# Row halves for attention scores, 32x32 transposes on VectorE, expert tables in sections, and one block for all stages

## What is computed

```python
def token_diffusion(x, Wqk, Wv, Wo, tau):            # 16 heads of 16
    qk = (x @ Wqk).reshape(b, n, H, dh).transpose(0, 2, 1, 3)
    v = (x @ Wv).reshape(b, n, H, dh).transpose(0, 2, 1, 3)
    dot = einsum('bhnd,bhmd->bhnm', qk, qk)
    q2 = sum(qk * qk, axis=-1)
    logits = (2.0 * dot - q2[..., :, None] - q2[..., None, :]) / sqrt(dh) * tau
    out = einsum('bhnm,bhmd->bhnd', softmax(logits), v)
    return out.transpose(0, 2, 1, 3).reshape(b, n, d) @ Wo
# channel_diffusion: the same over channels, 8 heads of 32
x = x + token_diffusion(layernorm(x), ...) * gamma1
x = x + channel_diffusion(layernorm(x), ...) * gamma2
# experts: top 2 of 8 by softmax(x @ w_router); 256 -> 1024 -> gelu -> 256
# whole: x = x + layernorm(attention(layernorm(x))); x = x + layernorm(experts(layernorm(x)))
```

## Time and profile before

| | us |
|---|---|
| median of 3 runs | 1127.04 (1125.57 to 1129.49) |
| the profiled execution | 1118.23 |
| its span on the core | 1116.4 |
| PE busy of the span | 1032.4 (92%) |
| ACT, DVE, POOL busy | 721.1, 671.4, 384.5 |

### The profile page before, as it was taken

How to read it: one execution, slowest core, us unless ns; L and a number is a source line. 1 busy time by engine, 2 the same in 40 slices (tenths; PEclk the granted TensorE clock), 3 DMA queues, 4 the chain that set the end, 5 groups by cost and what they waited for, 6 DMA issues and landing times. The chain is left out here.

```text
span 1116.4 us, 17406 instructions
## 1 busy us (share of the span) xinstructions
PE 1032.4 (92%) x5756; PEld 702.8 (63%) x5756; DVE 671.4 (60%) x1902; ACT 721.1 (65%) x1106; POOL 384.5 (34%) x353
## 2 busy tenths in 40 slices
PE   5899999999999999998899996999999999989966
PEld 3234545555455455544588875888888888878842
DVE  5225265454735645354785777677677776679927
ACT  2797767667776766666655662676677766768804
POOL 5121030513323141224426243444433443254315
PEclk9899999999999999999999987999999999989989
DMA  7673816427082542832433133334443344446456
GB/s 267 133 246 61 264 31 204 122 84 256 18 261 73 174 150 69 275 148 91 147 100 115 62 135 123 124 133 148 147 161 119 138 143 142 151 143 224 149 215 256
DMA packets 48960, 167.47 MB, mean 150 GB/s; under 512 B 10160, under 2 KB 16688, under 8 KB 42864
## 3 DMA queue, kind: packets, MB, share of 16 engines
q1 hardware_dynamic: 38170, 136.94, 36.9%
q0 software_dynamic: 10560, 29.14, 8.2%
q10 hardware_dynamic: 150, 0.41, 0.2%
HBM read 102.74 MB, written 63.70 MB: 149 GB/s over the span
## 5 line engine op out<-in xcount | busy, mean ns | idle before, releaser
L589 ACT ACTIVATE E<-PS,VV 128x1024 f32<-128x1024 f32 x256 | 271.6, 1119 | 73.7 <-PE PS L974 72.6
L1737 PE MATMUL PH<-XP,W1P 128*128 128x512 f32 (+1 forms) x1104 | 233.1, 369 | 4.9 <-DVE HP L1678 4.5
L1737 PEld LDWEIGHTS PH<-XP,W1P 128*128 128x128 f32 x1104 | 185.8, 192 | 44.5 <-DVE HP L1678 8.1
L974 PE MATMUL PS<-OPB,OPA 102*128 102x512 bf16 x512 | 137.9, 386 | 11.4 <-DMA OPB<-norm_parts 5.7
L1678 DVE TENSOR_TENSOR HP<-PH,HP 128x512 fp32r<-128x512 f32 x156 | 106.7, 686 | 64.8 <-ACT HP L1584 64.3
L957 PE MATMUL PO<-E,VA 128*32 128x512 f32 x1024 | 143.5, 610 | 0.0
L1579 ACT ACTIVATE PH<-PH,B 128x512 f32<-128x512 f32 (+1 forms) x184 | 107.5, 596 | 53.9 <-PE PH L1737 44.9
L1502 POOL DMA_INDIRECT choice_rows<-Y,DI x78 | 79.3, 1016 | 182.3 <-DVE Y L1635 160.8
L974 PEld LDWEIGHTS PS<-OPB,OPA 102*128 102x128 bf16 x512 | 37.7, 98 | 155.4 <-ACT E L589 68.7
L1570 ACT CAST W2P<-WG 128x512 fp32r<-128x512 f32 x92 | 56.9, 621 | 103.6 <-PE PB L1768 63.6
L462 POOL DMA_INDIRECT expert_rows<-PAY,SLOT x64 | 62.7, 979 | 157.5 <-issue 80.1
(11 more groups left out here) (254 smaller groups left out, 1611.2 us busy)
## 6 DMA issues: line engine op xcount, KB each, us to landing
expert_rows<-ZERO SPq DMA_DIRECT2D x8, 4160.0 KB, 12.8
WG<-experts SPq DMA_DIRECT2D x23, 1152.0 KB, 5.1
WG<-experts SPq DMA_DIRECT2D x23, 1028.0 KB, 5.2
OPB<-q_parts SPq DMA_DIRECT2D x192, 64.0 KB
YC<-choice_rows SPq DMA_DIRECT2D x8, 1024.0 KB, 13.0
q_parts<-QP SPq DMA_DIRECT2D x48, 128.0 KB
OPA<-q_parts SPq DMA_DIRECT2D x31, 192.0 KB
X<-x SPq DMA_DIRECT2D x8, 512.0 KB, 11.1
```

Source lines behind the costliest of these rows:

```text
L589: a.activation(E[:, s % 2, h, :, :], PS[:, u % 2, :, :], ACT.Exp, scale=vec("tau_t")[:, 4 * (s // 2) + h:4 * (s // 2) + h + 1]).then_inc(e ...
L974: ins = t.matmul(PS[:, u % 2, jc, :], OPA[0:KA, m, key:key + P], OPB[0:KA, m, hh * N:hh * N + N], start=True, stop=True)
L1737: last = m.matmul(PH[:, u % BANKS, at:at + w], W1P[:, a, k * HID + c * P:k * HID + c * P + P], XP[:, o, k, 0:w], start=(k == 0 and (a, o) ...
```

## The change

Five things are changed together.

1. Scores: q and the norms are split in two parts of fp32r (round-off kept by the second part) in place of three of bf16. A head then needs 52 rows, and `OPA`/`OPB` hold two heads on top of each other, one in rows 0 to 51, one in rows 64 to 115. A unit is now one pair of heads for one block of keys: two matmuls, in the two row halves of the array, into two banks of `PS`; ACT takes the exponential in two instructions of 512 columns.
2. The result of attention is transposed on DVE in blocks of 32x32 (`v.transpose`), divided, and transposed back, into `OTN`; `untok` on PE, `ontok` on PE and ACT are gone. The rows of Wo are loaded in another order (8 small DMAs) to suit. `proj` stays at position 5.
3. `BEGUN` is 7 in place of 5, in two stages (5 known, then 2 more by `begin` of batch B-2, in slots 18 to 21); `fill_begun` and `fill_tables` are generators, one section for each slot, `tables` in slots 73 to 81 (9 sections). The steps of the last batch in `TAIL_AT` are spread over slots up to 81 in place of 52.
4. Stage 3 is in the block of stages 1 and 2, with no barrier between; SP waits for the last rows of stage 2 itself.
5. In stage 3 there are ten pieces (the first and the last batch in halves), two of the sums and five of the last additions are on POOL, roots are taken for groups of pieces, and the matmuls on constants are gone.

```diff
-BEGUN = -(-(2 * N * (B - 2) - NE * (2 * SUB - 1)) // (2 * SUB))
+KNOWN = [-(-(2 * N * b - NE * (2 * SUB - 1)) // (2 * SUB)) for b in (B - 2, B - 1)]
+BEGUN = KNOWN[-1]
-POST_AT = {2: ['residual', 'untok0'], 3: ['untok1'], 4: ['ontok'], 5: ['proj'], 6: ['z2'], 8: ['x2t'], 9: ['qkc'], 10: ['gram'],
+POST_AT = {1: ['untok0'], 2: ['residual', 'untok1'], 5: ['proj'], 6: ['z2'], 8: ['x2t'], 9: ['qkc'], 10: ['gram'],
...
-           52: [('tables', B - 1)]}
+           71: [('prefix', B - 1)], **{k: [('tables', B - 1)] for k in range(73, 82)}}
...
             def att(b, par, pos, first):          # ACT
-                for i in range(2):
-                    h = 2 * (pos % 2) + i
-                    u = 4 * s + h
+                for jc in range(2):
+                    u = 4 * s + 2 * (pos % 2) + jc
                     act.wait_ge(s_full, UNITS * b + u + 1)
-                    a.activation(E[:, s % 2, h, :, :], PS[:, u % 2, :, :], ACT.Exp,
-                                 scale=...).then_inc(e_ready, 1)
+                    for r in range(2):
+                        h = 2 * (pos % 2) + r
+                        ins = a.activation(E[:, s % 2, h, jc, :], PS[:, u % 2, r, :], ACT.Exp, scale=...)
+                    ins.then_inc(e_ready, 1)
...
             def att(b, par, pos, first):          # PE
-                    for jc in range(2):
-                        key = hh * N + (2 * (s % 2) + jc) * P
-                        ins = t.matmul(PS[:, u % 2, jc, :], OPA[0:KA, m, key:key + P], OPB[0:KA, m, hh * N:hh * N + N],
+                    key = (2 * (s % 2) + jc) * P
+                    for r in range(2):
+                        at = HALF_ROWS * r
+                        ins = t.matmul(PS[:, u % 2, r, :], OPA[at:at + KA, m, pair, key:key + P], OPB[at:at + KA, m, pair, :],
                                        start=True, stop=True)
...
-                    pre.did(v.tensor_tensor(QR[:, m, :], QF[:, m, :], QP[:, m, 0, :], ALU.subtract))
-                    pre.did(v.tensor_copy(QP[:, m, 1, :], QR[:, m, :]))
-                    v.tensor_tensor(QP[:, m, 2, :], QR[:, m, :], QP[:, m, 1, :], ALU.subtract).then_inc(qp_ready, 1)
+                    v.tensor_tensor(QP[:, m, 1, :], QF[:, m, :], QP[:, m, 0, :].bitcast(f32), ALU.subtract).then_inc(qp_ready, 1)
...
+                    for r in range(2):            # untok on DVE
+                        post.did(v.transpose(TK[:, r, :], OT[:, 2 * m + r, :]))
+                    post.did(v.reciprocal(REC[:, :, :], blocks[:, :, :, DH]))
+                    for r in range(2):
+                        post.did(v.tensor_tensor(TN[:, m, :]...[:, r], blocks[:, r, :, 0:DH], REC[:, r, :]..., ALU.mult))
+                    v.transpose(OTN[:, m, :], TN[:, m, :]).then_inc(otn_ready, 1)
...
-        stage3(nc, make, X, const, ys, out)
+            last = stage3(nc, make(apart), X, const, HALF..., PB, ys, out, y_sent, y_rows)
...
+    PIECES = [(0, 0, 2), (0, 2, 2)] + [(b, 0, C) for b in range(1, B - 1)] + [(B - 1, 0, 2), (B - 1, 2, 2)]
+    BY_PE, BY_POOL = (0, 1, 2, 4, 5, 7, 8, 9), (3, 6)
+    ROOTS = [(0, 1), (2,), (3, 4), (5,), (6, 7), (8, 9)]
+    POOL_ADDS = (0, 1, 2, 3, 6)
-    WARM_UPS = 16
...
+        for r in range(2):                        # SP, in place of POOL and the barrier
+            sp.wait_ge(y_sent[r], y_rows[r])
```

530 lines of the change are left out of this document (290 added, 240 removed).

## The result

The changed kernel is slower. Beside each other on one chip it took 1147.9 us in the median (1143.5 to 1148.3, 4 runs) and the kernel before 1126.3 (1123.9 to 1129.5): a ratio of 1.0172, 95% interval 1.0136 to 1.0209. Repeated later on two chips it came to 1.0029 (0.9997 to 1.0061) and 1.0182 (1.0127 to 1.0236). On two of the three the loss is clear, on the third it can't be told from no change; so part of it depends on the chip. The prediction was 1064 us, a ratio of 0.944.

What follows compares the result with a forecast made beforehand. PE was taken to bound stage 1, with waits mattering in expert units 0 to 4. Gains of 41 (stage 1), 13 (tables) and 9 (end) sum to 63 us, taking the 1127.0 median to 1064 us; range 1040 to 1094.

Steps and rivals of the forecast that it cites:

- The score group at 0.53: Stage 1: a position's four score matmuls, paired in row halves, take 0.53 us with a switch in place of 0.87.
- one switch of 0.10: Stage 1 scores: changing the array's tiling mode costs PE about 0.10 us, paid once more behind a position's scores.
- a gain of 3: Batch 0 of stage 1: five positions with PE work gain 0.34 us each, the others a tenth; 3 us.
- "I take no change" for ACT: Stage 1: four exponentials of 512 columns cost 1.96 to 2.36 us, two of 1024 cost 2.1; no change.
- the rival "ACT and DVE take over": Stage 1: exponentials 0.59 us apart and DVE waits cut the batch gain to 2, whole gain 39, 1088 us; chance 0.17.
- The rule "the larger of PE's and ACT's work": Stage 1: each position takes the larger of both engines' work; batch sums 66.1 us before, 59.65 after.
- A clock under 1.00 in stage 1: Sign of a wrong forecast: a granted clock under 1.00 would say PE's idle shares cost more than themselves; no size.
- `OTN` on DVE, "covered by 2 us": Stage 1: DVE's about 12 us from the end of `chan` fit within PE's some 14 us to `proj`.
- The tables at -13: Expert units: tables in sections, with seven known units, cut waits and low clock; gain 13 us, bounds 0 and 22.
- the waits I had left 5.1: Around the tables in the expert units: PE waits of 2.6 + 0.6 + 1.9 us remain, 5.1 in all.
- The end at -9: Last stage: first issue to end 35.5 us in place of 43.3, with 1.5 for the barrier; gain 9, bounds 4 and 12.
- The "slower" rival: Stage 1 scores: row halves expose weight loads, four scores cost 1.6 us in place of 0.87, kernel 1177 us; chance 0.05.

Runs made afterwards that it cites:

- that with one exponential: Scores alone changed, but one exponential of 1024 columns for both heads of a pair, the second taking the first's scale; against the kernel before: 1119.9 us, ratio 1.0001.
- with them behind PAY: Block transposes alone, with the last batch's transposes behind the addition, statistics and normalization that make PAY, the input of `z3t0`; against the kernel before: 0.9948.
- the trace without gaps: Second trace of the unchanged changed kernel, without PE's unexplained gaps in expert unit 4; ratio to the kernel before 1.0029, traced execution 1131.2 us.

## Why the prediction was wrong, point by point

- **The score group at 0.53** was mis-sized: 0.66 measured. The halves do run side by side (starts 2 to 5 ns apart), that part was right. I counted one switch of 0.10; there are two, 0.11 for the first 32-bit unit, and 0.05 to 0.10 in the row behind. Where PE is the longer a position gains 0.11 to 0.16, and a batch gained 1 us, not 5.4. Batch 0, where I had a gain of 3, took 4.4 longer (4.1 with the scores alone).
- **"I take no change" for ACT** is the step that failed most. The bounds were 1.96 to 2.36 and I took 2.1, by the spacing of copies. Exponentials start 0.57 to 0.59 apart, 2.3 to 2.4 a position. Worth 12.4 us over stage 1 with PE's work unchanged. By itself that is the rival "ACT and DVE take over", but I had priced it as a gain left over of 2 us a batch; with the true score group nothing was left over.
- **The rule "the larger of PE's and ACT's work"** held for the transposes in the middle batches, which gave 2.0 to 3.1 of 2.8 us. That its sum for the kernel before came out at 66.1 of 66.35 was in part luck: by position it has 3.3 where 2.40 was measured (1), 4.6 where 5.30 was (2), 2.6 where 3.42 was (7), and the errors cancel. A list that is only right in sum says little of what a position gains.
- **A clock under 1.00 in stage 1** was named only as a sign. It came about once a batch, at positions 13 and 14, behind positions in which PE waits:

```profile
322.00:330.00 8.00, 6.68 (x28) 3.19 (x25) 5.10 (x38) 6.69 (x16) 1.05 (x1) 0.66 0.86 341
```

  A mean of 0.66 is a mix of the two levels, 2.4 and 1.2 GHz. Batches with such a drop took 1.4 to 3 us more than those without, in the kernel with the scores alone (67.8 to 69.4 against 66.4) and in that with one exponential (66.9 against 65.3). The kernel before had none from 36 us to 486. That PE's waits bring the drop is likely, not shown: the kernel with only the exponentials split waits too (10.1 us for `E`, where before has 5.6) and kept 1.00 in all its middle batches.
- **`OTN` on DVE, "covered by 2 us"**: true in the middle batches. In the last one, which the prediction treated as any other, the transposes stand in the chain to `z3t0`: 9.4 us of wait, and a clock of 0.80 behind it. How much of the 9.6 us by which that batch grew is theirs isn't settled: 5.4 with the transposes alone, 1.7 with them behind PAY on another chip. I had not looked at `LAST_AT`'s order, which puts `chan_norm` two positions earlier.
- **The tables at -13**: -4.9 in units 0 to 6 by themselves, and +7.5 by a drain that I had no row for (5.2 in the changed kernel, whose stores end later). Of the waits I had left 5.1; with the tables alone those for `HP` are 10.4, in the changed kernel, with the transposes of the last batch on DVE too, 15.4 to 19.4. In the trace without gaps that made the seven units 222.2 in place of 223.0, so the part gained nothing there.
- **The end at -9**: 51.6 became 48.2 where it stands alone. The start gained 3.7 (first sum 5.8 us behind the last issue in place of 9.5) and the sums 3.0 (24.7 in place of 27.7). The time behind the last sum grew by 3.3, from 9.6 to 12.9; the prediction left it out. It had 35.5 us from the first load to the end in place of 43.3; 42.0 were measured.
- **The "slower" rival** was the wrong mechanism. Exposed loads at 1.6 us a group didn't occur. What made the kernel slower were the split of the exponentials (12.4 us by itself), the last batch of stage 1 (9.6), the drain (5.2) and, where they come, the gaps (some 10 in unit 4). I had given the first a chance only as a smaller gain, and the others none.

## What to carry to other kernels

Price an instruction by a row of its own operation: a copy and an exponential with a scale per partition differ by 0.08 to 0.09 us at 512 columns, and 512 of these are 40 us. Splitting an instruction to suit another engine's layout has to be paid by the engine that splits, and it shows wherever that engine is the longer, even at 65% busy. Work taken from the bounding engine is only a gain where it wasn't filling a wait: look at the first and last pass of a loop by itself. Measure a change of mode at both sides of a group, and keep long groups. Before a stretch of one trace is blamed on a change, look whether other kernels from the same chip have it too.

## What the runs showed of the hardware that was not expected

- Two matmuls of 512 columns in the two row halves take 0.216 us together in 16 bits and 0.227 in 32 bits, the same as one over 102 rows; each change of form costs 0.10 and the first 32-bit unit behind it 0.11 (measured between these forms alone).
- POOL's drain at the end of a block took 1.1 to 1.7 us or 9.2, and which of them went with the order of indirect transfers 360 to 450 us earlier in all twenty traces.
- PE can issue a few matmuls at a time for 10 us with no wait that the profile shows, in two traces of three of the same kernel. In the second layer all eight traces of two chips have such gaps, none of the ten of three other chips.
- An ACT instruction of 128x512 starts 0.48 us behind the last one as a copy, 0.57 as an exponential with a scale per partition, 0.66 as a product and sum with a scale and a bias per partition.
- DVE's block transpose of 128x512 takes 0.65 us, 0.71 for the one that ends a chain.
